# Two attention layers and an MLP: the first layer's key evictions and masks go from VectorE to ScalarE, and the block norms' inverse roots become an iteration on VectorE

## The reference

```python
# layer 0, per batch: channels are rows, 512 columns are the sequence; 16 heads of 16 channels
q, k, v = Wq @ x + bq, Wk @ ctx + bk, Wv @ ctx + bv
attn = softmax(where(kv_mask, (q * scale) @ k, -inf))
mean, ex2 = attn @ v, attn @ (v * v)
std = sqrt(relu(ex2 - mean * mean))
x = (masked_instance_norm(x, mask) * std + mean) * mask
# block, per batch: 256 rows of 512 features, 16 heads of 32
h = layernorm(x) ; x = x + attention(h, h, self mask) @ w_ao + b_ao
h = layernorm(x) ; x = x + attention(h, ctx, cross mask) @ w_co + b_co
h = layernorm(x) ; x = x + gelu(h @ w1 + b1) @ w2 + b2
# layernorm(x) = (x - mean) / sqrt(var + 1e-5) * scale + bias
```

## Time and profile before

| | |
|---|---|
| time before, median of 3 | 1849.71 us (1848.66 to 1852.59) |
| profiled execution, its own time | 1844.77 us |
| its span, first to last instruction | 1843.0 us |
| TensorE busy / VectorE busy / ScalarE busy / GpSimd busy | 94% / 75% / 59% / 19% |
| mean granted clock of TensorE | 0.978 |
| layer 0 | about 0 to 700 us |
| attention stage | about 700 to 1440 us |
| MLP | about 1440 to 1843 us |

### The profile page before, as it was taken

The page is one execution under the profiler, slowest core; times in us unless marked ns, Lnnn a source line. Parts: engine busy times, 40 slices in busy tenths (PEclk is TensorE's granted clock), DMA queues, the critical chain, the costliest instruction groups (busy, mean ns, idle before and its releaser), DMA issues. The chain is left out here.

```text
span 1843.0 us, 34424 instructions
## 1 busy us (share of the span) xinstructions
PE 1726.7 (94%) x12371; PEld 1199.2 (65%) x12371; DVE 1373.1 (75%) x2843; ACT 1083.6 (59%) x2422; POOL 354.1 (19%) x427
## 2 busy tenths in 40 slices
PE   8999999999999997899989998999999599999998
PEld 4443334343333344788778777788887499999997
DVE  6879898898989745899898998899999553333322
ACT  2666666665767556777867777777777451111111
POOL 0003021121203131323222222222222130000000
PEclk9999999999999998999999999999999799999999
DMA  3101011010110212222232533333332140000000
GB/s 108 36 17 49 27 37 50 15 49 16 48 28 13 97 44 77 70 70 71 70 98 70 138 76 97 81 95 90 95 98 70 58 132 12 11 13 14 14 14 15
DMA packets 76504, 105.03 MB, mean 57 GB/s; under 512 B 21440, under 2 KB 36672, under 8 KB 76224
## 3 DMA queue, kind: packets, MB, share of 16 engines
q1 hardware_dynamic: 65856, 82.08, 16.2%
q0 software_dynamic: 8192, 16.79, 3.7%
q10 hardware_dynamic: 2304, 4.20, 0.8%
HBM read 39.55 MB, written 4.72 MB: 24 GB/s over the span
## 5 line engine op out<-in xcount | busy, mean ns | idle before, releaser
L530 DVE TENSOR_REDUCE nmax<-ps 128x2 f32<-128x1024 f32 x256 | 311.3, 1220 | 88.3 <-PE ps L397 86.7
L711 ACT ACTIVATE prob<-ps 128x1024 f32<-128x1024 f32 x256 | 261.7, 1022 | 192.8 <-PE ps L409 191.7
L1466 ACT ACTIVATE at_prob<-at_t,at_nmax 128x256 f32<-128x256 f32 x512 | 256.4, 505 | 108.4 <-DVE at_nmax L1269 99.3
L424 PE MATMUL ps<-prob,v 128*64 128x512 f32 x1024 | 279.1, 624 | 0.0
L1269 DVE CUSTOM_DVE_ANT_0 at_t<-at_t,at_off 128x256 f32<-128x256 f32 x512 | 236.6, 499 | 8.8
L1788 ACT ACTIVATE mlp_h<-ps,b 128x256 f32<-128x256 f32 x128 | 53.7, 472 | 268.1 <-PE ps L1723 268.1
L1827 DVE CAST mlp_h_hi<-mlp_h 128x512 fp32r<-128x512 f32 x64 | 29.8, 465 | 219.8 <-ACT mlp_h L1788 219.8
L1624 POOL TENSOR_TENSOR at_low<-at_low,at_high 128x512 fp32r<-128x512 f32 x64 | 85.5, 1336 | 500.2 <-DVE at_high L1295 500.2
L1100 PE MATMUL ps<-ident,at_prob 128*128 128x128 f32 x1024 | 160.1, 280 | 1.0 <-ACT at_prob L1466 1.0
L1089 PE MATMUL ps<-at_k_stack,at_q_stack 96*128 96x256 f32 x512 | 119.8, 317 | 36.0 <-ACT at_prob L1466 30.9
L1723 PE MATMUL ps<-mlp_x_hi,mlp_w_hi 128*128 128x256 f32 x512 | 145.8, 285 | 6.6 <-DVE mlp_w_lo L1812 6.6
(11 more groups left out here) (208 smaller groups left out, 4343.4 us busy)
## 6 DMA issues: line engine op xcount, KB each, us to landing
at_k_stack<-at_high SPq DMA_DIRECT2D x256, 64.0 KB, 2.5
at_q_stack<-at_high SPq DMA_DIRECT2D x128, 64.0 KB, 2.7
at_q_stack<-at_high POOLq DMA_DIRECT2D x128, 64.0 KB, 2.4
at_q_stack<-at_low SPq DMA_DIRECT2D x128, 64.0 KB, 2.1
at_k_stack<-at_low POOLq DMA_DIRECT2D x128, 64.0 KB, 2.3
mlp_w_in<-in_w SPq DMA_DIRECT2D x32, 256.0 KB, 3.1
c_in<-in_ctx SPq DMA_DIRECT2D x8, 512.0 KB, 4.3
X<-in_x SPq DMA_DIRECT2D x8, 512.0 KB, 5.1
```

Source lines behind the costliest of these rows:

```text
L424: mm = eng.matmul(ps[2 * QD * k:2 * QD * (k + 1), VB, :], v[:, c, HG * G + 2 * p + k, :], prob[:, M % PROBS, k, :], start=(c == 0), stop=( ...
L530: eng.tensor_reduce(nmax[:, n % 2, j, 2 * p:2 * p + 2], ps[:, at:at + 2, :], AX, ALU.max, negate=True).then_inc(s_max, 1)
L711: eng.activation(prob[:, M % PROBS, :, :], ps[:, ST:ST + 2, :], ACT.Exp).then_inc(s_exp, 1)
L1466: ins = eng.activation(prob[:, m % 2, i, :], t[:, p, i, :], ACT.Exp, scale=-1.0, bias=nmax[:, m % 4, i:i + 1], accum_out=z[:, T % 2, j, 2 ...
```

## The change

It has two parts. In layer 0 the first part of the keys (`high_k`) and the masks (`masks`) become ScalarE activations: `high_k(w+1)` right behind the exponential of step 5, `masks(b+1)` behind that of step 7 in the groups w % 4 == 2, and both ahead of `take_q(0)` at the start. VectorE keeps the rest (`rest_k`), which now waits for ScalarE's `k1`, and `low_k` of a batch's first group waits for `far`. `masks` waits for `last_mask` of three batches before through a semaphore of its own.

In the block, ScalarE's `roots` and VectorE's `reciprocals` go. `inverse_root_step` gets the inverse root on VectorE: a guess by an integer shift and a subtraction on the bits (part 0), then three rounds of three small operations (parts 1 to 3), each waiting for the one before. Lots 1 to 3 have part 0 in step 9 and the rounds in steps 10, 11 and 12; lot 0 has them in groups 26 and 27 (steps -47, -46, -41 and -40).

```diff
     every_batch(eng, padded)
+
+
+def inverse_root_step(eng, links, part, var, y, u):
+
+    def linked(ins):
+        ins.then_inc(links.sem, 1)
+        eng.wait_ge(links.sem, links.after())
+
+    if part == 0:
+        linked(eng.tensor_scalar(y.bitcast(I32), var.bitcast(I32), 1, None, ALU.logical_shift_right))
+        linked(eng.tensor_scalar(y.bitcast(I32), y.bitcast(I32), -1, ROOT_GUESS, ALU.mult, ALU.add))
+    else:
+        linked(eng.tensor_tensor(u, y, y, ALU.mult))
+        linked(eng.scalar_tensor_tensor(out=u, in0=u, scalar=-0.5, in1=var, op0=ALU.mult, op1=ALU.mult))
+        linked(eng.scalar_tensor_tensor(out=var if part == 3 else y, in0=u, scalar=1.5, in1=y, op0=ALU.add, op1=ALU.mult))
...
-        def masks(b):
-
-            if b == 1:
-                eng.wait_ge(s_bits, DMA)
-            eng.tensor_copy(mask[b % 3][:], m_in[:, b, :]).then_inc(s_mask, 1)
-            eng.wait_ge(s_mask, b + 1)
-            if b:
-                eng.wait_ge(s_k2, NG * b)
-            eng.tensor_scalar(far[:], mask[b % 3][:], row[:, FAR_AT:FAR_AT + 1], row[:, FAR_OFF:FAR_OFF + 1],
-                              ALU.mult, ALU.add).then_inc(links.sem, 1)
-            eng.wait_ge(links.sem, links.after())
-
-        def high_k(n):
-            made(eng, "k", n)
-            if n >= RING:
-                eng.wait_ge(s_st, 8 * (n - RING) + 8)
-            eng.tensor_scalar(k1[:, n % RING, :], bank_of("k", n), b0[:, 1, n % NG:n % NG + 1], None, ALU.add)\
-               .then_inc(s_k1, 1)
+        def rest_k(n):
             eng.wait_ge(s_k1, n + 1)
...
             taken(eng, "k", n)
+            if n % NG == 0:
+                eng.wait_ge(s_far, n // NG + 1)
             eng.scalar_tensor_tensor(out=k2[:, n % RING, :], in0=raw_k[:], scalar=row[:, IS_LOW:IS_LOW + 1], in1=far[:],
...
             eng.wait_ge(s_fin, FINISH * (b + 1))
-            eng.tensor_tensor(X[:, b, h, :], X[:, b, h, :], mask[b % 3][:], ALU.mult).then_inc(links.sem, 1)
-            eng.wait_ge(links.sem, links.after())
+            eng.tensor_tensor(X[:, b, h, :], X[:, b, h, :], mask[b % 3][:], ALU.mult).then_inc(s_masked, 1)
+            eng.wait_ge(s_masked, SB * b + h + 1)
             eng.bn_stats(six[:], X[:, b, h, :]).then_inc(links.sem, 1)
...
         eng.tensor_scalar(b0[:, 0, :], b0[:, 0, :], float(HD0) ** -0.5, None, ALU.mult).then_inc(s_b0, 1)
-        eng.wait_ge(s_first_bits, DMA)
-        masks(0)
-        high_k(0)
+        rest_k(0)
         low_k(0)
...
                         both_q(w + 1)
                     if s == 5:
-                        high_k(w + 1)
+                        rest_k(w + 1)
                     if s == 6:
                         low_k(w + 1)
...
                 b = w // NG
                 if w % NG == 3 and b < NB:
-                    if s == 1 and b + 1 < NB:
-                        masks(b + 1)
                     if s in (2, 4):
                         masked_x(b, s // 2 - 1)
...
+        def masks(b):
+
+            eng.wait_ge(s_bits if b else s_first_bits, DMA)
+            if b >= 3:
+                eng.wait_ge(s_masked, SB * (b - 2))
+            eng.activation(mask[b % 3][:], m_in[:, b, :], ACT.Copy).then_inc(s_mask, 1)
+            if b:
+                eng.wait_ge(s_k2, NG * b)
+            eng.wait_ge(s_mask, b + 1)
+            eng.activation(far[:], mask[b % 3][:], ACT.Identity, bias=row[:, FAR_OFF:FAR_OFF + 1],
+                           scale=row[:, FAR_AT:FAR_AT + 1]).then_inc(s_far, 1)
+
+        def high_k(n):
+
+            made(eng, "k", n)
+            if n >= RING:
+                eng.wait_ge(s_st, 8 * (n - RING) + 8)
+            eng.activation(k1[:, n % RING, :], bank_of("k", n), ACT.Identity, bias=b0[:, 1, n % NG:n % NG + 1])\
+               .then_inc(s_k1, 1)
+
         def take_q(n):
...
         eng.wait_ge(s_b0, 1)
         eng.activation(loaded[:], b0[:, 0, 0:1], ACT.Identity)
+        masks(0)
+        high_k(0)
         take_q(0)
         second_q(0)
...
                 if 0 <= M < 8 * GROUPS:
                     exponentials(M)
+                if s == 5 and w + 1 < GROUPS:
+                    high_k(w + 1)
+                if s == 7 and w % NG == 2 and b + 1 < NB:
+                    masks(b + 1)
                 if s in (0, 4) and 0 <= w - 2 < GROUPS:
                     take_values(2 * (w - 2) + s // 4)
...
             for layer, first, last in LOTS[n][1:]:
-                ins = eng.tensor_scalar(rstd[:, layer, first:last, :], moments[:, first:last, :, 1], EPS, None, ALU.add)
-            ins.then_inc(s_var, 1)
-
-        def reciprocals(n):
-            eng.wait_ge(s_root, n + 1)
-            for layer, first, last in LOTS[n][1:]:
-                ins = eng.reciprocal(rstd[:, layer, first:last, :], rstd[:, layer, first:last, :])
-            ins.then_inc(s_rstd, 1)
-            eng.wait_ge(s_rstd, n + 1)
+                eng.tensor_scalar(rstd[:, layer, first:last, :], moments[:, first:last, :, 1], EPS, None, ALU.add)\
+                   .then_inc(links.sem, 1)
+                eng.wait_ge(links.sem, links.after())
+            inverse_roots(n, 0)
+
+        def inverse_roots(n, part):
+
+            lot = LOTS[n][1:]
+            at = slice(SB * (NB * lot[0][0] + lot[0][1]), SB * (NB * lot[-1][0] + lot[-1][2]))
+            size = at.stop - at.start
+            inverse_root_step(eng, links, part, rstd[:].rearrange("p n b s -> p (n b s)")[:, at], guess[:, 0, 0:size],
+                              guess[:, 1, 0:size])
...
             step = 8 * (w - G0) + s
-            if step == -34:
+            if step == -47:
                 variances(0)
-            if step == -17:
-                reciprocals(0)
+            if step in (-46, -41, -40):
+                inverse_roots(0, (-46, -41, -40).index(step) + 1)
             if step == -6:
                 layer_norm(0)
...
                         if (run, m) == (of[0], 9):
                             variances(n)
-                        if (run, m) == (of[0], 11):
-                            reciprocals(n)
+                        if run == of[0] and m in (10, 11, 12):
+                            inverse_roots(n, m - 9)
                     if m in (11, 13) and run + 1 < RUNS:
                         values(run + 1, m // 2 - 5)
...
-        def roots(n):
-            eng.wait_ge(s_var, n + 1)
-            for layer, first, last in LOTS[n][1:]:
-                ins = eng.activation(rstd[:, layer, first:last, :], rstd[:, layer, first:last, :], ACT.Sqrt)
-            ins.then_inc(s_root, 1)
-
         def lead(w, s):
             step = 8 * (w - G0) + s
-            if step == -29:
-                roots(0)
             if step == -3:
```

More of the change, by code:

```diff
@@ L10 @@
 U8 = mybir.dt.uint8
+I32 = mybir.dt.int32
 ALU = mybir.AluOpType
@@ L32 @@
 NEVER = 3.0e38
+ROOT_GUESS = 0x5F3759DF
 DMA = 16
@@ L202, in layer0 @@
         s_mask = sem("mask")
+        s_far = sem("far")
+        s_masked = sem("masked")
         s_stat = sem("stat")
@@ L948, in attention @@
         h_raw = sb("h_raw", [P, 2, S])
-        six = g["six"]
+        six, guess = g["six"], g["guess"]
         masks, b_rows = (g["mask_self"], mask_cross), (g["b_self"], b_cross)
@@ L958, in attention @@
         s_ctx = sem("ctx")
-        s_var = sem("var")
-        s_root = sem("root")
-        s_rstd = sem("rstd")
         s_xn = sem("xn")
@@ L1607, in runs @@
                         load_weights(3)
-                    for n, of in enumerate(LOTS):
-                        if (run, m) == (of[0], 9):
-                            roots(n)
                     late(run, m)
@@ L1914, in build @@
             keep(attentions, "two", [P, 2])
+            keep(attentions, "guess", [P, 2, SB * NB])
             first, then = layer0(nc, d, g), attention(nc, d, g)
```

## The result

The changed kernel takes 1836.22 us (median of 6 runs, 1834.41 to 1840.29) against 1847.33 for the kernel before (6 runs, 1843.59 to 1852.59): ratio 0.994, 95% interval 0.9921 to 0.9959. Its profiled execution took 1837.26 of its own, against 1844.77 before.

A forecast was written before the change was run, and what follows sets the result against it. Layer 0 was taken as a ScalarE-TensorE ring with TensorE pacing item steps, the attention as bound by VectorE. Terms of -5.6 and -2.5 made -8.1, taking 1849.7 to 1841.6 us; range 1836.5 to 1850.5.

The forecast's parts named there:

- place 2: Third of a batch's four layer 0 groups: `k1` delays an exponential by 0.6 us, absorbed by an unmoved maxima wait; gain 0.
- both go: Attention runs 5 and 9: table loads and the low-clock stretch both disappear, gaining 1.1 and 1.7 us, together 2.8.
- Place 0: First of a batch's four layer 0 groups: `k2` ends earlier, gaining 0.75 us in six batches, 4.5 in all.
- Place 1: Second of a batch's four layer 0 groups: value item stops waiting for `raw_k`, 0.23 us in six batches, 1.4 in all.
- Place 3: Fourth of a batch's four layer 0 groups: the root's wait for `std_a` goes, 0.18 us in six batches, 1.1 in all.
- Rival B: Layer 0: VectorE reaches `x_lo` before GpSimd, maxima waits of 12.5 us shrink by some 5; result 1836.6, chance 0.12.
- First batch, +0.6, and group 1, +0.2: Layer 0's start: first batch lacks a maxima wait to absorb `k1`, costing 0.6 us; group 1's weight rounding adds 0.2.
- rival E: Attention: the low clock stays in runs 5 and 9, or comes elsewhere; +4 us, result 1845.6, chance 0.10.
- Run 3, +0.3: Attention run 3 keeps its two loads; the third round costs 0.6 us, less 0.2 for the small root; with rounding +0.3.
- Lot 0, +0.6: Layer 0, group 26 step 7 and group 27 step 0: the round before step 0's maxima costs 0.6 us.
- rival C: New small VectorE operations meet GpSimd, each costing 1.0 us more; 15 of them give +15, result 1856.6, chance 0.05.
- Rivals A and D: A: ScalarE uncovered at place 2, +6.6 us, chance 0.22; D: `k1` misses its gap in ordinary groups, +15, chance 0.06.

The follow-up runs named there:

- an experiment of their own: The kernel after with the masks put back on VectorE, the rest of the change kept: 1836.04 us, ratio 0.9947 against the kernel before.
- The wait on GpSimd: The kernel before, with GpSimd made to wait for VectorE's `x_lo` before its `mean_a` products at each batch's third group: 1843.81 us, ratio 0.9987.
- run 5: Not a follow-up: a numbered stretch of the attention stage, holding inverse roots; from its exponential of step 10 to the next stretch's first, 17.95 us before.
- run 9: Not a follow-up: a numbered stretch of the attention stage, holding inverse roots; from its exponential of step 10 to the next stretch's first, 18.33 us before.
- run 10: Not a follow-up: a numbered attention stretch that the forecast took as having no inverse roots; from its exponential of step 10 to the next stretch's first, 14.74 us before.
- the moved rounds: The kernel after with lot 0's inverse-root rounds three steps earlier and lots 1 to 3 in step 15: 1829.22 us, ratio 0.9913 against before.
- the kernel after with GpSimd's wait: The kernel after, with GpSimd made to wait for `x_lo` before its products at each batch's third group: 1835.65 us, ratio 0.9946 against before.
- batch 1: Follow-up runs on one chip: kernel before 1847.46 us, unchanged copy 1846.43, layer-0 part alone 1838.35, inverse roots alone 1846.16, whole change again 1836.47.

## Why the prediction was right and wrong, by its own steps

**In short.** The range was missed by a base that was too high, 1849.7 where six runs gave 1847.3, and by a term put at nothing: at place 2 the forecast took VectorE's 1.77 us for `x_lo` as fixed, and it is the outcome of a race that the change shifts, worth about 1 us by the rows and 2 by the medians. A third step failed in the other direction: in runs 5 and 9 "both go", loads and low clock, and the low clock did not: 0.3 longer with run 3, where 2.5 less was forecast. About 4 of the 11.1 us between the medians are found in no profile.

**Right.** Place 0: the wait for `k2` is gone, 0.65 per batch where 0.75 was worked out, and the moments' wait stayed. Place 1: 0.21 per batch (0.23). Place 3: 0.14 (0.18). The masks: 0, by the rows of an experiment of their own. ScalarE's `k1` took 0.68 and fitted its gap in plain groups. Lot 0's loads: taking them out gave nothing, 40.72 us for the two rows with the whole change and 40.77 with the layer-0 part alone, which keeps them. The small operations: 0.16 to 0.17, pitch 0.2, integer forms included. These terms make -6.0 in the table, against -6.95 forecast for the same rows.

**The base.** The last step, "the difference applies to it", added the forecast change to 1849.7, the median of three executions. All later medians of the kernel before, of six runs and more, lie at 1846.4 to 1848.0. From 1847.4 the same sum gives 1839.3: 2.3 of the 5.4 us are this, an error of the base and not of the change.

**Place 2: "This wait does not move", "nothing is gained".** This step failed. Half of it held: where `x_lo` is free and GpSimd's products begin before +7.7, the row from place 2 takes 18.8 to 19.0 with `k1` on VectorE and 18.95 to 18.99 with it on ScalarE, so of ScalarE's 0.6 at most 0.2 is paid. What failed is to take the 1.77 of the earlier trace rows as fixed. It is the outcome of a race. VectorE reaches `x_lo` 6.91 us after the row's first exponential in before and 6.67 in after, always; GpSimd's products start between +6.4 and +8.2, as their DMA lands. In the profile of the earlier trace rows VectorE lost 4 of 6 times, in after 2 of 6. The prediction had both outcomes before it, the "1.5 in four batches and 0.6 in two", and took each as fixed. Rival B named this mechanism, with 0.12, and held against it that "`k1`'s move takes only 0.2 off that chain"; 0.24 is enough where the two starts lie within tenths of each other. Group 6, where GpSimd starts at +6.8 in both kernels, before and then after, VectorE and GpSimd in each:

```profile
145.81 1.77 DVE L485 TENSOR_TENSOR x_lo<-X,x_hi 128x512 fp32r<-128x512 f32 x1
145.70 3.02 POOL L823 TENSOR_TENSOR mean_a<-mean_in,rz 128x512 f32<-128x512 f32 x2 [16.00 <-DMA second<-v_out]
```

```profile
145.16 0.69 DVE L504 TENSOR_TENSOR x_lo<-X,x_hi 128x512 fp32r<-128x512 f32 x1
145.28 3.45 POOL L849 TENSOR_TENSOR mean_a<-mean_in,rz 128x512 f32<-128x512 f32 x2 [16.00 <-DMA second<-v_out]
```

The wait on GpSimd shows the race's price in before: 2.6 us on the median (0.2 to 4.6), and half of its spread. In after it is 0.6 to 0.8. Four profiles of before have 4, 3, 4 and 3 caught, two of after 2 and 1. By the medians, then, the race gives the change 1.8 to 2 us. By the rows it gives less, since there is a second such meeting. Where GpSimd's products start late, from +7.4 on in the kernel after, `x_lo` is free but the rest of the context, `c_lo`, 1.7 later on VectorE, is caught. Group 14 of the kernel after, where they started at +8.18 and the row took 19.49:

```profile
307.44 1.60 DVE L509 TENSOR_TENSOR c_lo<-c_in,c_hi 128x512 fp32r<-128x512 f32 x1
307.21 2.98 POOL L849 TENSOR_TENSOR mean_a<-mean_in,rz 128x512 f32<-128x512 f32 x2 [17.05 <-DMA second<-v_out]
```

In the two profiles of after `c_lo` takes 1.2 to 1.6 in three of six batches, and the five rows from place 2 without lot 0 sum to 96.5 on average, where the four profiles of before have 97.4: 0.9 less. The Trainium skill (SBUF — State Buffer, SBUF: two separate sides) has the exclusion of such a VectorE operation and a GpSimd one for a whole instruction; these traces agree, 1.77 against 0.68 for `x_lo` by who started first.

**First batch, +0.6, and group 1, +0.2.** Both were over-counted: the two rows take 39.10 before and after. The exponentials do come late (2.44 and 2.36 against 1.87 and 2.22), but the item that follows has room (2.10 instead of 2.58) and a later wait shrinks from 2.94 to 2.61. The step looked for cover only in a wait for maxima, and gave nothing for VectorE's relief in these rows.

**Runs 5 and 9: "Both go", loads and low clock.** This step failed. The loads went; the low clock stayed in run 5, and it came and went in run 9 with either kernel. The forecast window of 16.6 for run 9 is near, 16.79 in four of five profiles, but the loads give the same, 16.75, in the one profile of six where the clock stays up. Loads on ScalarE and rounds on VectorE cost run 9 the same 2.0 to 2.1 over run 10's 14.7, and a fall of the clock another 1.1 to 1.6. In run 5 the clock falls in every profile of either kind, 17.62 to 17.97, where 16.8 was forecast. That is rival E. The forecast compared a window without the fall to one with it, and laid the fall to the loads. But VectorE has 0.6 us of gaps in 14.74, so the rounds make stalls of their own. Weight loads of TensorE in run 9 of the kernel after, waiting for what stands behind a round, and three windows around the fall:

```profile
1167.30 0.30 PEld L1112 LDWEIGHTS ps<-at_k_stack,at_q_stack 96*128 96x128 f32 x2 [1.13 <-ACT at_prob L1492]
...
1169.75 0.19 PEld L1184 LDWEIGHTS ps<-at_wv_hi,at_c_hi 128*128 128x128 f32 x1 [1.20 <-DVE at_v L1329]
```

```profile
1166.00:1168.00 2.00, 1.30 (x9) 0.87 (x7) 1.86 (x10) 1.84 (x6) 1.70 (x4) 1.00 0.53 121
1168.00:1170.00 2.00, 1.07 (x20) 0.63 (x19) 1.90 (x10) 1.43 (x6) 0.00 (x0) 1.00 0.73 191
1170.00:1172.00 2.00, 2.00 (x6) 1.59 (x6) 1.97 (x8) 0.80 (x3) 0.00 (x0) 0.52 0.34 86
```

TensorE is busy 1.30 and 1.07 of 2.00, and then the granted clock is 0.52: near the 1.2 GHz level. These stalls alone do not decide it. The same three windows in the second profile of the same kernel have the same busy time before, and no fall:

```profile
1165.31:1167.31 2.00, 1.30 (x9) 0.87 (x7) 1.86 (x10) 1.86 (x6) 1.70 (x4) 1.00 0.53 122
1167.31:1169.31 2.00, 1.08 (x20) 0.65 (x18) 1.90 (x10) 1.43 (x6) 0.00 (x0) 1.00 0.68 177
1169.31:1171.31 2.00, 2.00 (x13) 1.72 (x13) 1.97 (x8) 0.82 (x3) 0.00 (x0) 1.00 0.39 98
```

What does show that the work in steps 9 to 12 brings the falls is the moved rounds: in step 15 neither run has such a stretch in three profiles, and run 5 is 3.3 to 3.5 shorter than in the kernel after's profile, run 9 3.2 shorter than where it had fallen and 2.1 than where it had not.

**Run 3, +0.3.** It cost more, 0.7 against the profiled before (48.52 and 47.82). Run 3 of the kernel before varies with a low clock of its own: 46.5 in the two of four profiles where the clock of its window is 1.00, 47.8 and 48.0 where it is 0.91. After the change it is 48.5 and 48.6, with 0.91 in every profile. The term is 0.5 to 2, 1.4 on average, and part of it may be that the clock now falls every time.

**Lot 0, +0.6, and rival C.** The row with both late rounds and a caught `x_lo` is 20.29 against 19.67 for one without rounds: 0.6. Where `x_lo` is free, VectorE comes to the round of step 7 while GpSimd's next products (549.34 to 551.86) still run and is caught, the rival's mechanism, at this one place. VectorE in the kernel after with GpSimd's wait:

```profile
550.58 1.30 DVE L102 TENSOR_TENSOR guess<-guess 128x10 f32<-128x10 f32 x1
551.92 0.17 DVE L103 SCALAR_TENSOR_TENSOR guess<-guess,rstd 128x10 f32<-128x10 f32 x1
```

1.30 for the first operation where the next takes 0.17, and a row of 20.53 against 18.97: 1.5. With all of them in steps 1 and 2 of group 26 the rounds cost nothing, 18.97.

**Rivals A and D** did not come true: of ScalarE's delays only the 0.2 and 0.25 told above are paid, and VectorE's relief is worth as much or more in the same rows. Rival B's 1836.6 is the number nearest to the result, but not by its account: it wanted the waits for maxima to shrink by 5, and they shrank by 2.8; the rest of the way is the base.

**The sum.** Four profiled executions of before took 1844.8, 1845.1, 1845.7 and 1841.4, mean 1844.2; two of after 1837.3 and 1836.9, 7.1 less, where the forecast had 8.1. By stages, on average: 1.0 up to layer 0's first exponential (40.5 to 43.3 us in all profiles, whatever the kernel; nothing shows that the change does this), 6.3 in layer 0 behind it (5.6 forecast), 0.4 in the attention's runs 0 to 14 (2.5 forecast; runs 3, 5 and 9 alone are 0.3 longer, 141.6 before and 141.9 in four profiles with both parts), and 0.5 more behind them. In layer 0 these are -6.1 on average for places 0, 1 and 3 and lot 0's old place, -0.9 at place 2 without lot 0 and +0.7 in the row with lot 0's rounds. So in the profiles the race does not make up for what the attention did not give. That the 1836.7 worked out for the profiled execution lies within 0.6 of the 1837.26 of after's is luck: between these two layer 0 gave 6.4 where 5.6 was forecast, and runs 0 to 14 1.4 where 2.5 was.

The medians are 11.1 apart, and 11.0 in batch 1. None of the profiled executions of before reached its median of 1846.4 to 1848.0, while those of after lie at theirs. So of the 5.4 us under the forecast, 2.3 to 2.4 are the base, and the other 3 belong to what makes executions of before longer than those profiled. The race is part of it, by the medians with GpSimd's wait and by the halved spread. The granted clock goes with the length of an execution, but its mean is 0.977 for both kernels, so it does not tell them apart. The rest stays open: the change does something to it that no row here names.

## What to carry to other kernels

When an operation in a profile takes two lengths (`x_lo` 0.68 or 1.77), look at every instance and at how far apart the two engines' starts are: a chain that becomes 0.24 earlier can decide such a race, and one wait on the engine that can afford it settles it; then look at what the delayed engine meets next, as GpSimd does `c_lo`. Work moved to the engine that is last costs its own time and what the idle TensorE behind it loses in clock; the same work in a step where that engine waits anyway cost nothing that shows here and gave 6 to 7 us, more than the attention part of the change had promised. And take the base of a forecast from more than three runs, or give its error a place in the range.

## What was not expected of the hardware

- TensorE's granted clock: the same instructions in run 9 went with 1.00 in some profiles and with 0.90 in others (rounds: 16.79 and 17.92 us; loads: 16.75 and 18.3), and with TensorE busy for the same time before. Whether the clock falls in a given execution is not set by the program alone.
- VectorE's integer shift and its integer multiply-add on 128x8 take 0.17 us each, as the floating-point forms do.
- A 128x512 subtraction on VectorE takes 0.68 or 1.77, by whether it or GpSimd's product began first, even where the two starts are 0.05 apart (caught), or 0.01 with VectorE ahead (free, the kernel after's second profile, group 26).
- A mean granted clock of 0.975 or less and one of 0.978 or more went with 1849.2 and 1844.1 us of one and the same kernel, on average over 16 and 24 executions.
